# One pass of a tuned kernel changed: probabilities transposed in 32x32 blocks by VectorE and put in place by DMA, instead of by TensorE

## The reference, cut to what matters

```python
q = (query @ wq) ...; k = (key @ wk) ...; v = (value @ wv) ...      # then rope on q and k
raw = jnp.einsum('bhqd,bhkd->bhqk', q, k) / scale
attn = jax.nn.softmax(raw + mask, axis=-1)
out = jnp.einsum('bhqk,bhkd->bhqd', attn, v)
x = x + jnp.tanh(g_xattn[0]) * (out @ wo)
```

## Time and profile before

| | |
|---|---|
| median of 3 runs | 795.31 us (793.71 to 796.48) |
| the profiled execution's own time | 795.32 us |
| its span, first to last instruction | 793.5 us |
| attention units 0 to 31, about | 48 to 574 us of the span |
| DMA traffic | 71.02 MB, 77778 packets |

### The profile page before, as it was taken

How to read it: one execution, slowest core, us unless ns; L and a number is a source line. 1 busy time by engine, 2 the same in 40 slices (tenths; PEclk the granted TensorE clock), 3 DMA queues, 4 the chain that set the end, 5 groups by cost and what they waited for, 6 DMA issues and landing times.

```text
span 793.5 us, 13550 instructions
## 1 busy us (share of the span) xinstructions
PE 780.8 (98%) x4940; PEld 638.8 (81%) x4957; DVE 541.4 (68%) x1043; ACT 437.7 (55%) x824; POOL 498.0 (63%) x430
## 2 busy tenths in 40 slices
PE   8999999999999999999999999999999999999998
PEld 7888888888888888888888888888765777777776
DVE  6857866666676545466655555555899987998874
ACT  5754455444454434444454433333579898888773
POOL 2797477645556764475676456546457885887753
PEclk9999999999999999999999999999999999999999
DMA  9312533432523131952113111267273413213101
GB/s 335 107 66 68 139 80 81 133 97 72 148 77 89 40 102 58 47 147 77 63 40 105 43 51 27 36 64 277 82 191 95 107 48 81 74 49 80 48 16 40
DMA packets 77778, 71.02 MB, mean 89 GB/s; under 512 B 51552, under 2 KB 52800, under 8 KB 77328
## 3 DMA queue, kind: packets, MB, share of 16 engines
q1 hardware_dynamic: 77424, 69.82, 34.1%
q10 hardware_dynamic: 288, 0.33, 0.1%
HBM read 49.04 MB, written 6.34 MB: 70 GB/s over the span
## 4 chain that ended last, share of the span: by engine, by line
PE 87%; DVE 4%; DMA 4%; POOL 2%; ACT 2%; issue 1%; another core or an unknown queue 1%; SPq 0%; DVEq 0%
PE bank L81 11%; PE bank L83 10%; PE bank L82 10%; PE bank L554 7%; PE bank L577 6%; PE bank L572 6%; PE bank L573 6%; PE bank L667 4%; PE bank L1645 4%; PE bank L1631 3%; PE bank L1597 2%; PE bank L1568 2%; PE bank L1576 2%; PE bank L1621 2%; DMA w_out<-w_quant 2%; PE bank L1622 2%
## 5 line engine op out<-in xcount | busy, mean ns | idle before, releaser
L970 DVE SCALAR_TENSOR_TENSOR x_res<-bank,gate,x_res 128x512 f32<-128x512 f32 x128 | 95.4, 747 | 74.0 <-PE bank L577 73.4
L1231 POOL TENSOR_TENSOR prob<-prob,row_inv 128x512 f32<-128x512 f32 x32 | 33.4, 1044 | 166.1 <-DVE row_inv L966 159.5
L1217 POOL TENSOR_TENSOR rope_swap<-rope_swap,trig 128x512 f32<-128x512 f32 x80 | 104.0, 1300 | 30.6 <-ACT rope_swap L737 30.3
L736 ACT COPY rope_swap<-bank 64x512 f32<-64x512 f32 x80 | 46.7, 584 | 110.3 <-DVE rope_cos L941 110.2
L941 DVE TENSOR_TENSOR rope_cos<-bank,trig 128x512 f32<-128x512 f32 x80 | 54.2, 678 | 76.5 <-PE bank L83 71.4
L572 PE MATMUL bank<-wo_hi,oT_hi 128*128 128x512 f32 x256 | 101.7, 397 | 1.2 <-DVE x_res L970 0.6
L81 PE MATMUL bank<-xnT_hi,wq_hi 128*128 128x512 f32 x252 | 101.5, 403 | 0.0
L573 PE MATMUL bank<-wo_lo,oT_hi 128*128 128x512 f32 x256 | 100.8, 394 | 0.0
L83 PE MATMUL bank<-xnT_hi,wq_lo 128*128 128x512 f32 x252 | 99.9, 396 | 0.0
L82 PE MATMUL bank<-xnT_lo,wq_hi 128*128 128x512 f32 x252 | 99.5, 395 | 0.0
L1223 POOL TENSOR_TENSOR q_rope<-rope_cos,rope_swap 128x512 f32<-128x512 f32 x64 | 84.2, 1315 | 5.0
(11 more groups left out here) (273 smaller groups left out, 1936.2 us busy)
## 6 DMA issues: line engine op xcount, KB each, us to landing
wq_raw<-in_wq_tiles SPq DMA_DIRECT2D x16, 512.0 KB, 3.8
wo_raw<-in_L_xattn_wo SPq DMA_DIRECT2D x16, 512.0 KB, 3.9
xn<-in_L_ffn_Wd SPq DMA_DIRECT2D x16, 256.0 KB, 3.6
b_ctx<-in_ctx SPq DMA_DIRECT2D x32, 128.0 KB, 2.6
b_k_twice<-b_qk_hi SPq DMA_DIRECT2D x32, 128.0 KB, 2.4
w_T_dram<-w_out SPq DMA_DIRECT2D x28, 128.0 KB, 3.1
w_T<-w_T_dram SPq DMA_DIRECT2D x2, 1376.0 KB, 19.9
xn<-in_L_ffn_Wg SPq DMA_DIRECT2D x10, 256.0 KB, 3.0
```

What stands on the lines that cost most here:

```text
L970: dve.scalar_tensor_tensor(out=K.x[:, t, :], in0=wo_ps[t % 2][:, :], scalar=K.gate[:, 0:1], in1=K.x[:, t, :], op0=ALU.mult, op1=ALU.add).t ...
L1217: pool.tensor_tensor(out=sw, in0=sw, in1=sin_b, op=ALU.mult).then_inc(s_rope, 1)
```

## The change

In units 1 to 30 TensorE no longer transposes the probabilities and ScalarE no longer copies them. Units 0 and 31 (`ON_PE`) are left as they were. VectorE turns `prob[U % 2]` in 32 x 32 blocks into a new tile `blocks` (`turn_blocks(U + 1)`, behind the first item and `second_piece` of slot U). SyncE stores `blocks` (256 KB) to device memory (`blocks_out`, at the start of step V = 2U), goes on with the load, the store and the turn of that step, waits until the store has landed and the values of the unit before have been used, and brings the blocks back with four DMAs of 64 KB, one for each 32 partitions of `probT` (`blocks_in`). The load of wo moves one step later, behind `blocks_in` (`load_wo_behind`). `probT` has another order of its columns, so that a row of the AV products is read in four runs of 32. A semaphore is shared with the last block's stores, and the scratch space for GpSimd's DMAs gets smaller.

```diff
+QB = 32
+NQ = P // QB
-        probT = sb("probT", [P, UT, 2 * S])
+        probT = sb("probT", [P, NQ, UT, QB])
+        blocks = sb("blocks", [P, NQ, UT, QB])
+        blocks_dram = [nc.dram_tensor(f"blocks_dram{i}", (P, NQ, UT, QB), F32, kind="Internal").ap() for i in range(2)]
+        ON_PE = (0, 2 * NPAIR - 1)
+        def n_turned(n):
+            return sum(1 if U in ON_PE else NQ * 16 for U in range(n))
...
+            def blocks_out(U):
+                sp.wait_ge(s_probT, U + 1)
+                sp.dma_start(blocks_dram[U % 2], blocks[:, :, :, :]).then_inc(s_to_dram, 16)
+
+            def blocks_in(U):
+                sp.wait_ge(s_av, U)
+                sp.wait_ge(s_to_dram, 16 * U)
+                for i in range(NQ):
+                    sp.dma_start(probT[i * QB:(i + 1) * QB, :, :, :].rearrange("c j t r -> c j (t r)"),
+                                 blocks_dram[U % 2][:, i, :, :].rearrange("(j c) t r -> c j (t r)", j=NQ)).then_inc(s_probT_sb, 16)
+
+            def load_wo_behind(m, u):
+                if u == 3 and m + 2 < NPAIR:
+                    sp.wait_ge(s_wo_lo[(m + 1) % 2], NQP * ((m + 1) // 2 + 1))
+                    load_wo(m + 2)
...
+                U = V // 2
+                turned = V % 2 == 0 and U not in ON_PE
+                if turned:
+                    blocks_out(U)
                 if (p := piece_at(V + 1)) is not None and p > 0:
                     load_piece(p)
                 if (p := piece_at(V - 3)) is not None:
                     store_piece(p)
                 if (p := piece_at(V - 2)) is not None:
                     turn_piece(p)
+                if turned:
+                    blocks_in(U)
+                if V > 0:
+                    load_wo_behind((V - 1) // 4, (V - 1) % 4)
                 next_weights(V // 4, V % 4)
...
-                pe.wait_ge(s_prob, U + 1)
-                for tl in range(UT):
-                    mm = pe.transpose(trans[:, tl * P:(tl + 1) * P], prob[u][:, tl], K.ident[:, :])
-                mm.then_inc(s_probT, 1)
+                if U in ON_PE:
+                    pe.wait_ge(s_prob, U + 1)
+                    for tl in range(UT):
+                        mm = pe.transpose(trans[:, tl * P:(tl + 1) * P], prob[u][:, tl], K.ident[:, :])
+                    mm.then_inc(s_probT, 1)
...
-                pe.wait_ge(s_probT_sb, U + 1)
+                pe.wait_ge(s_probT_sb, n_turned(U + 1))
...
-                                       probT[rows, tl, :], start=True, stop=True)
+                                       probT[rows, :, tl, :], start=True, stop=True)
...
-                    if U > 0:
+                    if U == 2 * NPAIR - 1:
                         probT_copy(U)
...
+            def turn_blocks(U):
+                dve.wait_ge(s_prob, U + 1)
+                if U > 1:
+                    dve.wait_ge(s_to_dram, 16 * (U - 1))
+                flat = prob[U % 2][:, :, :, :].rearrange("p t b k -> p t (b k)").rearrange("p t (i c) -> p i t c", c=QB)
+                dve.transpose(blocks[:, :, :, :], flat).then_inc(s_probT, 1)
...
                     if k == 0:
                         second_piece(U)
+                        turn_blocks(U + 1)
```

More of the change, by code:

```diff
@@ L180, in attention_block @@
         s_probT_sb = sem("s_probT_sb")
+        s_to_dram = K.s_to_dram
         s_av = sem("s_av")
@@ L378, in next_weights @@
                     load_wq(m + 4, m % 2)
-                if u == 3 and m + 2 < NPAIR:
-                    sp.wait_ge(s_wo_lo[(m + 1) % 2], NQP * ((m + 1) // 2 + 1))
-                    load_wo(m + 2)
             sp.wait_ge(s_wk_first, 2)
@@ L787, in probT_copy @@
                 act.wait_ge(s_probT, U + 1)
-                act.copy(probT[:, :, :], trans[:, :].rearrange("p (t n) -> p t n", t=UT)).then_inc(s_probT_sb, 1)
+                act.copy(probT[:, :, :, :], trans[:, :].rearrange("p (t j r) -> p j t r", t=UT, j=NQ)).then_inc(s_probT_sb, 1)
             probT_copy(0)
@@ L1531, in last_programs @@
         s_y, s_res = sem("s_b_y"), sem("s_b_res")
-        s_store = [sem(f"s_b_store{i}") for i in range(2)]
+        s_store, stored = [K.s_to_dram, sem("s_b_store1")], [16 * (2 * NPAIR - 2), 0]
         def small_ps(t):
@@ L2260, in finish @@
                 dve.wait_ge(s_x3b, t + 1)
-                after(dve, s_store[i], 16 * (t // 2))
+                after(dve, s_store[i], stored[i] + 16 * (t // 2) if t > 1 else 0)
                 if t == NT - 1:
@@ L3243, in sync @@
             for i in range(2):
-                sp.wait_ge(s_store[i], 16 * (NT // 2))
+                sp.wait_ge(s_store[i], stored[i] + 16 * (NT // 2))
         programs.tensor, programs.vector, programs.scalar, programs.gpsimd, programs.sync = tensor, vector, scalar, gpsimd, sync
@@ L3274, in setup_block @@
     K.s_w_in = cx.sem("s_w_in")
+    K.s_to_dram = cx.sem("s_to_dram")
     K.stats, K.meanvar = cx.sb("f_stats", [P, NT, 6]), cx.sb("meanvar_ffn", [P, NT, 2])
@@ L3324 @@
     from concourse.bass_utils import run_bass_kernel_spmd
-    nc = bacc.Bacc("TRN2", target_bir_lowering=False, num_devices=1)
+    nc = bacc.Bacc("TRN2", target_bir_lowering=False, num_devices=1, dynamic_dma_scratch_size=8192)
     arrays, aps = {}, {}
```

## The result

The changed kernel takes 812.23 us (median of 4 runs, 812.11 to 813.74), the kernel before 795.89 on the same chip (793.71 to 797.28): a ratio of 1.0217, with a 95% interval of 1.0202 to 1.0232. It is slower by 2.2%. The profiled execution took 812.11 for a span of 810.0, 16.5 more than the span before.

The account below looks back on a forecast made before the run. TensorE, busy 98% of the span, was taken as the bound. The terms -11.9 + 1 + 4 + 12.3 + 1 + 0.5 + 7.3 = +14.2 on 795.31 gave 809.5 us, range 800 to 825.

Parts of the forecast that it names:

- What goes: TensorE's transposes, units 1 to 30: 27 x 0.44 = 11.9 us saved, nothing to win in units 28 to 30.
- The pass: VectorE's added 128x512 pass per unit: 0.69 us, not waiting for anything, cost 0; 1.24 us as the other estimate.
- An ordinary unit: Round trip through SyncE's queue: blocks back at 214.5, AV due at 216.2, so hidden by 1.7 us.
- the +1 for units 1 to 3: Two-item units give less cover, so units 1 to 3 miss by a few tenths: +1 us (0 to 3).
- every unit is late: Rival, chance 0.15: the trip takes 10.9 instead of 8.2, each of 24 three-item units loses 1 us, 833.
- (a) Unit 27: Blocks stand behind the last block's 17 loads in SyncE's queue; TensorE waits, +12.3 us (10.5 to 14).
- (b) Unit 17: Blocks stored behind unit 16's element-by-element weight scales land late and hold AV: +4 us (0 to 9).
- (c) The third scales: Scales going out in unit 28 lengthen TensorE's wait for GpSimd's wo share: +1 us, up to 9.
- (d) The end: Loads behind the loop now follow unit 30's blocks: base weights +0.5 us, context loads delaying unit 31 +7.3.
- Base +0.5: At the end, base weights land about when TensorE wants them: +0.5 us.
- Unit 31 +7.3: Context loads behind 5.28 MB delay ScalarE's copy of unit 31's probabilities; AV at 576.5, not 569.17: +7.3 (3 to 9).
- The clock: Rival, chance 0.18: clock falls to half in the holds of units 27 and 31, +3.9 us each, 813 to 817.

Follow-up runs that it names:

- f2: e4 with units 28, 29 and 30 transposed on TensorE too; 784.44 us, ratio 0.9855 to the kernel before.
- g1: The kernel before with transposes and copies of units 1 to 30 left out, nothing in their place; 788.73 us, ratio 0.9891.
- e1: The changed kernel with the 17 loads of the last block issued behind the blocks of unit 27; 800.98 us, ratio 1.0045.
- e6: The changed kernel with the first two weights' scale stores moved from step 32 to step 56; 824.33 us, a single run.
- e7: e1 with context tiles ahead of w_T, base weights in step 55, first two weights' scale stores in step 28; 794.05 us, ratio 0.9959.
- e3: The changed kernel with unit 17 transposed on TensorE and copied by ScalarE as before; 807.25 us, ratio 1.0126.
- e2: The changed kernel with base weights loaded in step 57 and context tiles loaded ahead of w_T; 806.73 us, ratio 1.0113.
- f1: The changed kernel with 48 unread 128x512 matmuls between scores and AV in unit 27; 810.84 us, ratio 1.0178.
- e5: The changed kernel with 90 transposes of the identity between scores and AV in unit 27; 814.38 us, ratio 1.0224.
- e4: The changed kernel with the edits of e1, e2 and e3 together; 786.94 us, ratio 0.9868 to the kernel before.
- f3: e4 once more, on the same chip as f2; 784.61 us, ratio 0.9852 to the kernel before.

## Why the prediction was right

The forecast was 809.5, and 812.23 was measured, inside the range of 800 to 825 and the bounds of 802 to 817. The holds came where they were forecast, but one mechanism was a rival's, and that the time fits so well is in part luck. Term by term, from the profile:

- **What goes.** Forecast -11.9, measured -12.2 by the steps. The 0.25 more than 11.9 lie in units 29 and 30 and are not the transposes', since f2 has them too. That units 28 to 30 have nothing to win is shown twice, by g1 (left out) and by f2 (put back).
- **The pass.** Taken at 0.69, measured 0.706 (30 rows, 0.697 to 0.712), at the place I gave it. The estimate of 1.24 that I had from the Trainium skill (VectorE: DVE Perf Modes, The three transpose paths) does not hold: 512 columns in float32 take 2.3 times its 311 ns for 128x128 in bf16, not four times. The measurement decides.
- **An ordinary unit.** Hidden, as forecast, but with 3.7 us to spare where I had 1.7. Three prices were too high: the four issues (1.95, not 2.2), the landing of the last (1.9, not 2.4) and the microsecond for the turn ahead of them, which nothing shows. With the right ones the +1 for units 1 to 3 goes: they come at -0.43, -0.47 and -0.43. (In seven of the ten experiments with blocks unit 1 did wait for them, 0.3 to 0.5 us, so the low end of my 0 to 3 was right.) The rival "every unit is late" falls by the same rows.
- **(a) Unit 27.** Forecast 12.3, lost 11.43. The mechanism is shown by e1. It is smaller by prices alone: the 17 issues took 12.45 us (501.30 to 513.75) instead of 12.9, the store landed in 2.8 instead of 2.5, the four issues took 1.76 instead of 2.2, and the last landed 1.9 after its start instead of 2.4.
- **(b) Unit 17.** Forecast 4, lost 4.65, by the path forecast and one more. I had the blocks landing with the load behind the scales, at 336.8 in the times of before, 329.7 with the 7.1 us gained by then; they landed at 333.07, 3.4 later. The last DMA back started at 334.92, where 340.2 less 7.1 is 333.1. What I had not seen is that the turn ahead of them would be held just as long, and that TensorE's scores would be 2.21 late by GpSimd. Moving the stores takes it all away (e6, e7), moving unit 17 to TensorE takes most of it (e3).
- **(c) The third scales.** Forecast +1, measured 0: the steps of 28 to 30 less the clock are those of g1.
- **(d) The end.** Base +0.5, measured 0 in the sum, but the path was missed: TensorE did not wait for it, VectorE did, 2.49 us, and TensorE 2.35 us through VectorE. By itself that would have made AV 31 3.5 us late; the context's hold, which ends later, covers it. Unit 31 +7.3, measured 7.91, by the path forecast: context loads behind 5.28 MB, ScalarE's splits behind these, probT_copy behind the splits. With unit 30 7.38 late the forecast's 571.5 for the first tile becomes 578.9; the split began at 578.87. e2 shows that the two loads together are the cause.
- **The clock.** I gave it 0.18 as a rival and left it out of the sum; this is the step that failed: the term was put at nothing. It fell in unit 27 (2.05), in unit 17 (AV 2.08 in place of 1.16, and 1.47 lost up to unit 18) and around unit 31 (1.2 behind AV): 4.7 us. The price of 3.9 a hold was too high, since the clock came back 4.7 us after the restart, before AV and the item were through at half speed; for that the short stops counted as well, which no rival had. The 4.7 us are less than the 7.8 the rival gave for two holds, and the time lies below its 813 to 817. The Trainium skill (TensorE: Matmul & The Clock Gate, What's actually happening) says that the clock is held back unless activity releases it; the trace agrees for the hold of 11.36 us, and f1 agrees by the reverse. That the smaller stops in units 17 and 31 cost what I put down to the clock is read from the clock rows and was not tested.

Forecast +14.2, plus 4.7 for the clock, less 1, 1 and 0.5 for the three terms that were nothing, plus 0.65 in unit 17, less 0.87 in 27, plus 0.61 in 31, less 0.28 more saved: +16.5, the difference of the spans. The forecast came within 3 us because terms too high made up for half of the clock; that is luck.

**What stays open.** How much the scale stores cost is not settled. The steps of units 17 and 18 add up to -1.9 where the stores stand elsewhere (e6, e7). With the stores in step 32 and the blocks of unit 17 in the queue they add up to +5.2 in the changed kernel, 6.8 in e1, 7.2 in e2, 4.5 in e5 and 6.8 in f1; with unit 17 on TensorE to -0.3 in e3, 1.3 in e4, 1.4 in f2 and -1.1 in f3, though e4 and f3 are one kernel; and to 4.2 in g1, which has no blocks. So the blocks of unit 17 are a large part, and the rest differs from profile to profile. Roughly, it goes with the time that the turn behind the scales took to land. Without blocks of unit 17 that was 17.2 us in f3, 19.0 in e3, 19.1 in f2, 19.7 in e4 and 19.9 in g1, for steps of -1.1, -0.3, 1.4, 1.3 and 4.2; with them 18.0 in e5, 18.6 in the changed kernel, 19.2 in e1 and 20.3 in f1, for 4.5, 5.2, 6.8 and 6.8. VectorE waits for that turn, and the next store goes out behind it, at 331.51 in the changed kernel and at 330.27 in f3. What sets the landing was not found. In the changed kernel VectorE also stood idle for 4.13 us ahead of 324.87 and ScalarE for 2.62 ahead of 320.49, and what the profile names as their releaser had long been done or is no engine; what held them I do not know.

## What to carry to other kernels

Taking 0.44 us of work off the bound engine gave 0.44 us in each unit up to 27 that nothing else held, and the round trip was free where the queue was free; the loss came from three places where an in-order queue was already full, and from the clock behind them. So before giving a queue a deadline in each unit, list its long stretches (many issues, element-wise stores, megabytes) and either move these or leave those units as they were. A unit that need not go by the new path is the cheapest mend. And to the price of a hold of TensorE belongs the clock that it comes back with.

## What the runs showed of the hardware

- **Stores element by element.** Four stores of the scales, a few KB in packets of under 512 B (0.01 MB and 1656 of 1661 packets in 2 us), kept what was issued behind them for 12.3 to 18.9 us, where 2.0 to 3.0 is usual (changed kernel; 20.3 in e6). DMAs issued 9 us apart landed within 2.4 us of each other. The Trainium skill (DMA: Bandwidth & Descriptors, Queues, rings and completion order) says that each DMA engine serves its ring in order and that a transfer's count lands only behind that engine's earlier writes; the trace agrees in that what stood behind the small packets landed only when these were through; no run here tells the ring from the count.
- **The clock after a filling.** After 8.9 us of transposes the granted clock was 0.57 on average over the next 4 us, its lower level for most of them, while TensorE was busy (e5); after 11.2 us of 128x512 matmuls it did not fall (f1). With nothing in the hold it was at 0.50 from 511 on and full again by 525 (changed kernel).
- **Short stops.** The granted clock was 0.50 between 334 and 340 in the changed kernel, with TensorE's waits of 2.21 and 2.43 us there; it had fallen after the first and before the second. In g1 it was at 0.50 from 341 on, after a wait of 2.97. I had expected a fall only in the long holds.
